# A perceiver layer on one core: split tail products, single-step layer norms, another setup, and a last group in two token halves

## The reference, cut to what matters

```python
x = x + xattn(_layernorm(x), ctx_768, ...)   # 16 heads of 64: q from x, k and v from the context
x = x + attn(_layernorm(x), ...)             # 16 heads of 16 inside a batch
x = x + ffn(_layernorm(x), ...)              # r * (relu(xk @ Wk.T)**2 @ Wv.T), r = sigmoid(xr @ Wr.T)
```

## Time and profile before

| what | value |
| --- | --- |
| median of three runs | 902.88 us |
| the profiled execution: own time, span in the trace | 905.87 us, 903.4 us |
| PE, weight loads | 822.6 us (91%), 641.3 us (71%) |
| DVE, ACT, POOL | 579.5 us (64%), 549.5 us (61%), 430.7 us (48%) |
| mean granted TensorE clock | 0.972 |
| first score, first score of group 1's part of the list | 44.98 us, 123.71 us |
| end of the last AC job on TensorE, end | about 826 us, 903.4 us |

### The profile page before, as it was taken

The page is one execution under the profiler, slowest core; times in us unless marked ns, Lnnn a source line. Parts: engine busy times, 40 slices in busy tenths (PEclk is TensorE's granted clock), DMA queues, the critical chain, the costliest instruction groups (busy, mean ns, idle before and its releaser), DMA issues.

```text
span 903.4 us, 20097 instructions
## 1 busy us (share of the span) xinstructions
PE 822.6 (91%) x7414; PEld 641.3 (71%) x7414; DVE 579.5 (64%) x1674; ACT 549.5 (61%) x1338; POOL 430.7 (48%) x661
## 2 busy tenths in 40 slices
PE   5699989998999989998999989998999999897653
PEld 3487758785878758786878768785878768684532
DVE  2553475769576775778576775778576756682344
ACT  1566865688467865677467865677467864673111
POOL 1036733755256723755266724755266724764001
PEclk9889999999999999999999999999999999999767
DMA  7301110001000110102010110002000110000000
GB/s 208 123 12 48 25 48 13 25 25 50 22 25 25 28 56 12 26 24 64 9 25 25 36 48 13 25 24 71 1 25 25 37 36 13 25 12 24 1 1 12
DMA packets 49232, 30.49 MB, mean 34 GB/s; under 512 B 22896, under 2 KB 48304, under 8 KB 49136
## 3 DMA queue, kind: packets, MB, share of 16 engines
q1 hardware_dynamic: 49136, 29.22, 11.9%
HBM read 26.85 MB, written 2.10 MB: 32 GB/s over the span
## 4 chain that ended last, share of the span: by engine, by line
PE 67%; DVE 14%; issue 7%; POOL 6%; ACT 5%; SPq 1%; DMA 1%; POOLq 0%; DVEq 0%; ACTq 0%
PE score L661 15%; PE post L755 5%; PE pre L573 5%; DVE qk_t L1123 5%; PE probT L670 4%; PE ac_tail L685 4%; POOL prT_l L356 4%; PE post L764 3%; DVE qk_l L1118 3%; PE ac_main L691 3%; PE ac_main L695 3%; PE aux L624 2%; PE ac_main L692 2%; PE post L738 2%; PE post L744 2%
## 5 line engine op out<-in xcount | busy, mean ns | idle before, releaser
L491 POOL TENSOR_SCALAR pr<-pr,rsum,poison 128x257 f32<-128x257 f32 x256 | 166.6, 660 | 233.6 <-DVE rsum L1148 233.5
L356 POOL TENSOR_TENSOR prT_l<-prT,prT_h 128x512 fp32r<-128x512 f32 x128 | 169.1, 1324 | 126.6 <-ACT prT_h L945 126.6
L928 ACT ACTIVATE pr<-sm,nmx 128x257 f32<-128x257 f32 x256 | 129.8, 509 | 83.8 <-DVE nmx L1142 83.4
L1142 DVE CUSTOM_DVE_ANT_0 sm<-score,mbias 128x257 f32<-128x257 f32 x256 | 106.2, 422 | 85.4 <-PE score L661 68.5
L937 ACT ACTIVATE prT<-probT 128x512 f32<-128x512 f32 x128 | 75.6, 590 | 44.9 <-PE probT L670 44.5
L661 PE MATMUL score<-cT_h,qk_h 128*128 128x258 f32 x256 | 89.6, 350 | 13.2 <-DVE qk_t L1123 12.9
L945 ACT ACTIVATE prT_h<-prT 128x512 fp32r<-128x512 f32 x128 | 80.7, 630 | 1.1
L670 PE MATMUL probT<-ident,pr 128*128 128x128 f32 x512 | 77.7, 274 | 3.4 <-POOL pr L491 2.6
L661 PE MATMUL score<-cT_h,qk_t 128*128 128x258 f32 x256 | 73.5, 287 | 0.0
L661 PE MATMUL score<-cT_l,qk_h 128*128 128x258 f32 x256 | 73.1, 285 | 0.0
L661 PE MATMUL score<-cT_h,qk_l 128*128 128x258 f32 x256 | 73.1, 285 | 0.0
(11 more groups left out here) (260 smaller groups left out, 2024.5 us busy)
## 6 DMA issues: line engine op xcount, KB each, us to landing
cx_in<-in_ctx_dram SPq DMA_DIRECT2D x64, 192.0 KB, 2.4
cx_in<-in_ctx_dram SPq DMA_DIRECT2D x64, 64.0 KB, 2.3
xn<-in_x_dram SPq DMA_DIRECT2D x8, 256.0 KB, 3.4
xb<-in_x_dram SPq DMA_DIRECT2D x8, 256.0 KB, 3.5
out_dram<-yo SPq DMA_DIRECT2D x8, 256.0 KB, 2.7
wq<-in_L_xattn_Wq_dram SPq DMA_DIRECT2D x1, 1024.0 KB, 5.1
wo<-in_L_xattn_Wo_dram SPq DMA_DIRECT2D x1, 1024.0 KB, 7.6
wqkv<-in_L_attn_W_qkv_dram SPq DMA_DIRECT2D x1, 768.0 KB, 8.8
```

What stands on the lines that cost most here:

```text
L356: eng.tensor_tensor(prT_l[:, :, cut], prT[:, :, cut], prT_h[:, :, cut], ALU.subtract).then_inc(prob_lower, 1)
L491: last = pool.tensor_scalar(p, p, rsum[:, j % 2, t:t + 1], poison[:, 0:1], ALU.mult, ALU.mult)
L928: act.activation(pr[j % 2][:, t, :], sm[:, t % 2, :], ACT.Exp, bias=nmx[:, j % 2, t:t + 1], scale=-1.0, accum_out=ssum[:, j % 2, t:t + 1]) ...
L1142: dve.tensor_tensor_reduce(sm[:, t % 2, :], score[t % 2][:, 0:NK], mbias[:], DH ** -0.5, BIG, ALU.add, ALU.min, nmx[:, j % 2, t:t + 1]).th ...
```

## The change

**Tails.** The tail channels are split as the main ones are. `c_hl` holds for each row 128 main channels (upper), 64 tail channels (upper), 64 tail channels (lower), 128 main channels (lower); its columns 128 to 255 are one stationary tile, so that a 512-column product gives the tail's upper part in the lower and its lower part in the upper 64 rows of ac_tail. ACT copies the rows 64 to 127 to `act_low`, and DVE adds the two in two pieces.

**Layer norm.** Twelve stages of one wait each, with a place in the list for each; the Newton step uses a scaled copy of the variance and takes one column at a time.

**Setup.** The transfers come in another order, small and large loads apart, the query weights in two halves. Products of the setup use further banks; the feed-forward weights are transposed in group 0 (`F0` to `F2`); K0 to K11 (there named `H`) stand in group 0's list among the first scores.

**Lists.** There are three of each: first group, middle groups, last group. In the last one the remainder of group 7 is cut in two token halves, `.0` (batches 0 to 3) and `.1`, with banks of their own. A product into a post bank waits for the last user of that bank.

```diff
+PE_LAST = (
...
+    "S2:7 S3:7 P1:6 AC:5 FR FK P0:7 AC:6 FV OT0.0 P1:7 OT1.0 WO.0 LT.1 AC:7 OT0.1 T2.0 OT1.1 QT.0 KT.0 WO.1 SC.0 VR.0 "
+    "T2.1 QT.1 KT.1 SC.1 VR.1 PT.0 PV.0 T4.0 PJ.0 PT.1 PV.1 T4.1 PJ.1 T3.0 T3.1 FR.0 FK.0 FR.1 FV.0 FK.1 FV.1").split()
...
-SETUP = "WK0 Q0 WK1 F0 Q1 WK2 F1 Q2 WK3 F2 Q3".split()
...
+SETUP = "WK0 WK1 XT WK2 WK3 Q0 LEFT Q1 CT0".split()
...
-LN_LINKS = 5 + 3 * NEWTON
+LN_LINKS = 5 + 2 * NEWTON
+LN_STAGES = LN_LINKS + 1
...
+        c_hl = [sb(f"c_hl{r}", [P, 2, 2 * DC], F32R) for r in range(2)]
+        UPPER, TAILS, LOWER = slice(0, P), slice(P, 2 * DC - P), slice(2 * DC - P, 2 * DC)
+        act_low = sb("act_low", [64, NH * NQ])
...
+        QK_SETUP_BANKS = [(score[0], score[1]), (post, probT), (ac_main, ac_tail), (post, probT), (ac_main, ac_tail), (post, pre)]
...
+        CLOSING_OT_BANKS = {"OT0.0": (post, pre), "OT1.0": (post, pre), "OT0.1": (score[0], score[1]), "OT1.1": (probT, ac_tail)}
+        CLOSING_BANKS = [(pre, post), (ac_main, aux, score[0], score[1], probT, ac_tail)]
...
+        SETUP_PRE_BANKS = {"XT": pre, "Q0": probT, "Q1": ac_main, "Q2": ac_tail, "Q3": pre}
...
             sp.dma_start(xn[:], token_rows(x_rows, 0)).then_inc(x_in, 16)
-            sp.dma_start(wq[:], Wq.rearrange("(k p) n -> p k n", p=P)).then_inc(wq_in, 16)
+            for n, v in ((G1, g1), (B1, be1)):
+                sp.dma_start(cols[:, n, :], column(v)).then_inc(ln1_in, 16)
...
-            for n, v in ((G1, g1), (B1, be1), (G2, g2), (B2, be2), (MUR, mur), (MUK, muk)):
+            wq_columns = Wq.rearrange("(k p) n -> p k n", p=P)
+            sp.dma_start(wq[:, :, 0:512], wq_columns[:, :, 0:512]).then_inc(wq_in, 16)
+            sp.dma_start(left_in[:, 0:DC], ctx_in[:, NKF, :]).then_inc(left_staged, 16)
+            sp.dma_start(left_in[:, DC:256], ctx_in[:, NKF, P:DC]).then_inc(left_staged, 16)
+            load_ctx(0, 0)
...
+            sp.dma_start(wq[:, :, 512:1024], wq_columns[:, :, 512:1024]).then_inc(wq_rest_in, 16)
...
             eng.wait_ge(c_upper, g * GB + j + 1)
-            eng.tensor_tensor(c_l[j % 2][:], cx_in[j % NCTX][:, :, 0:P], c_h[j % 2][:], ALU.subtract).then_inc(c_lower, 1)
+            c, src = c_hl[j % 2], cx_in[j % NCTX]
+            eng.tensor_tensor(c[:, :, DC:2 * P], src[:, :, P:DC], c[:, :, P:DC], ALU.subtract)
+            eng.tensor_tensor(c[:, :, LOWER], src[:, :, 0:P], c[:, :, UPPER], ALU.subtract).then_inc(c_lower, 1)
...
                 after(pe, acm_copied, g * GB + j)
                 after(pe, act_copied, g * GB + j)
 
-                pe.wait_ge(probT_copied, n)
-                for m in range(2):
-                    by_pair = prT[:, m, :].rearrange("p (n r x) -> p n r x", r=2, x=2 * NQ)
-                    for r in range(2):
-                        pe.matmul(ac_tail[r * 64:r * 64 + 64, 0:TOK], cx_in[j % NCTX][:, m, P:DC], by_pair[:, :, r, :],
-                                  start=(m == 0), stop=(m == 1))
                 pe.wait_ge(c_lower, g * GB + j + 1)
                 pe.wait_ge(prob_upper, n)
+                c = c_hl[j % 2]
                 for m in range(2):
-                    pe.matmul(ac_main[:], c_h[j % 2][:, m, :], prT_h[:, m, :], start=(m == 0), stop=False)
-                    pe.matmul(ac_main[:], c_l[j % 2][:, m, :], prT_h[:, m, :], start=False, stop=False)
+                    pe.matmul(ac_main[:], c[:, m, UPPER], prT_h[:, m, :], start=(m == 0), stop=False)
+                    pe.matmul(ac_main[:], c[:, m, LOWER], prT_h[:, m, :], start=False, stop=False)
+                    pe.matmul(ac_tail[:], c[:, m, TAILS], prT_h[:, m, :], start=(m == 0), stop=False)
                 pe.wait_ge(prob_lower, n)
                 for m in range(2):
-                    last = pe.matmul(ac_main[:], c_h[j % 2][:, m, :], prT_l[:, m, :], start=False, stop=(m == 1))
+                    pe.matmul(ac_main[:], c[:, m, UPPER], prT_l[:, m, :], start=False, stop=(m == 1))
+                    last = pe.matmul(ac_tail[:], c[:, m, TAILS], prT_l[:, m, :], start=False, stop=(m == 1))
                 last.then_inc(ac_done, 1)
...
                 act.wait_ge(probT_full, 2 * (g * GB + j) + half + 1)
...
-                    after(act, ac_done, g * GB + j)
+                after(act, prob_lower, 2 * (g * GB + j - 1) + half + 1)
                 act.activation(prT[:, :, half * 256:(half + 1) * 256], probT[:].rearrange("p (m c) -> p m c", m=2),
...
+                if half == 0:
+                    after(act, ac_done, g * GB + j)
                 cut = slice(half * 256, (half + 1) * 256)
                 act.activation(prT_h[:, :, cut], prT[:, :, cut], ACT.Copy).then_inc(prob_upper, 1)
...
-                act.activation(c_h[j % 2][:], cx_in[j % NCTX][:, :, 0:P], ACT.Copy).then_inc(c_upper, 1)
+                act.activation(c_hl[j % 2][:, :, 0:DC], cx_in[j % NCTX][:, :, 0:DC], ACT.Copy).then_inc(c_upper, 1)
 
             def weighed(g, j):
                 act.wait_ge(ac_done, g * GB + j + 1)
+                after(act, act_copied, g * GB + j)
+                act.activation(act_low[:], ac_tail[64:128], ACT.Copy).then_inc(tail_lower, 1)
                 act.activation(acm[:, :, j * NQ:(j + 1) * NQ], ac_main[:].rearrange("p (h q) -> p h q", q=NQ),
                                ACT.Copy).then_inc(acm_copied, 1)
...
+                w, y, q = lw[:, n, 0], lw[:, n, 1], lw[:, n, 2]
+                if stage > 0:
...
                 if stage == 0:
...
+                    for a in part:
+                        last = dve.bn_stats(st[:, n, a, :], src[:, a, :])
+                elif stage == 1:
...
-                    dve.bn_aggr(mv[:, n, 0, :], st[:, n, 0, :])
-                    dve.bn_aggr(mv[:, n, 1, :], st[:, n, 1, :]).then_inc(ln_link[n], 1)
-                elif stage < 4:
-                    if stage == 1:
-                        linked(2)
-                        dve.tensor_scalar(w, mv[:, n, :, 1], scale, shift, ALU.mult, ALU.add).then_inc(ln_link[n], 1)
-                        linked(3)
-                        dve.tensor_scalar(li[:, n, :], w.bitcast(I32), 1, None, ALU.logical_shift_right).then_inc(ln_link[n], 1)
-                        linked(4)
-                        dve.tensor_scalar(y.bitcast(I32), li[:, n, :], -1.0, RSQRT_SEED, ALU.mult, ALU.add).then_inc(ln_link[n], 1)
...
-                    dve.tensor_tensor(q, y, y, ALU.mult).then_inc(ln_link[n], 1)
-                    linked(i + 1)
-                    dve.scalar_tensor_tensor(out=q, in0=q, scalar=-0.5, in1=w, op0=ALU.mult, op1=ALU.mult).then_inc(ln_link[n], 1)
-                    linked(i + 2)
-                    dve.scalar_tensor_tensor(out=y, in0=q, scalar=1.5, in1=y, op0=ALU.add, op1=ALU.mult).then_inc(ln_link[n], 1)
...
+                elif stage == 2:
+                    dve.tensor_scalar(w[:, own], mv[:, n, own, 1], -0.5 * scale, -0.5 * shift, ALU.mult, ALU.add)
+                    last = dve.tensor_scalar(lw[:, n, 3, own], mv[:, n, own, 1], scale, shift, ALU.mult, ALU.add)
+                elif stage == 3:
+                    last = dve.tensor_scalar(li[:, n, own], lw[:, n, 3, own].bitcast(I32), 1, None, ALU.logical_shift_right)
+                elif stage == 4:
+                    last = dve.tensor_scalar(y[:, own].bitcast(I32), li[:, n, own], -1.0, RSQRT_SEED, ALU.mult, ALU.add)
...
+                elif stage % 2:
+                    for a in part:
+                        one = slice(a, a + 1)
+                        last = dve.scalar_tensor_tensor(out=q[:, one], in0=y[:, one], scalar=w[:, one], in1=y[:, one],
+                                                        op0=ALU.mult, op1=ALU.mult)
...
+                    last = dve.scalar_tensor_tensor(out=y[:, own], in0=q[:, own], scalar=1.5, in1=y[:, own], op0=ALU.add, op1=ALU.mult)
+                last.then_inc(link, 1)
...
-                dve.wait_ge(ac_done, g * GB + j + 1)
-                dve.tensor_copy(act_[:, :, j * NQ:(j + 1) * NQ],
-                                ac_tail[:, 0:TOK].rearrange("p (n q) -> p n q", q=NQ)).then_inc(act_copied, 1)
+                dve.wait_ge(tail_lower, g * GB + j + 1)
+                upper, lower = (t.rearrange("p (n r e q) -> p n r e q", r=2, e=2, q=NQ) for t in (ac_tail[0:64], act_low[:]))
+                for r in range(2):
+                    own = act_[r * 64:r * 64 + 64, :, j * NQ:(j + 1) * NQ].rearrange("p (n e) q -> p n e q", e=2)
+                    last = dve.tensor_tensor(own, upper[:, :, r], lower[:, :, r], ALU.add)
+                last.then_inc(act_copied, 1)
...
-                if j == 0 and t in FIRST_USE:
-                    pe.wait_ge(qk_split, g * N_QK + FIRST_USE[t])
+                first_use = FIRST_USE_0 if g == 0 else FIRST_USE
+                if j == 0 and t in first_use:
```

829 lines of the change are left out of this document (464 added, 365 removed), and 48 rows, old and new, of tables (ACT_FIRST, ACT_LAST, ACT_ORDER, DVE_FIRST).

## The result

The changed kernel takes 888.64 us (median of 4 runs, 886.88 to 890.68) against 902.69 (4 runs, 899.77 to 904.21): ratio 0.9854 [0.9833, 0.9874]. It is 1.5% faster, 14 us where 40 were forecast, and 863 lies 26 us too low. The profiled execution was the slowest of the four, 890.68 with a span of 888.6 (before: 905.87 and 903.4).

What follows compares the result with a forecast made beforehand. TensorE was taken to bound the middle, chains the start and end. From 905.87, -11.4 (tails), -7 (setup) and -23 (end) gave 864.5; median 861.5, plus 1.5 for waits: 863. Forecast 852 to 870 (chance 0.55), range with rivals 845 to 884.

Steps and rivals of the forecast that it cites:

- The tails: Weighing job (AC) after each score: ten 512-column products instead of mixed ones, 0.27 us less a batch, 1.6 a middle group.
- the lists and the layer norm: Middle groups: layer norm costed at 0; waits brought by other lists cost 0.2 us a group, 1.5 in seven groups.
- The lists also fill the waits: Rival: K products' 2.4 us of waits a group and the last group's 7.7 vanish; 845 us, chance 0.13.
- Slower: the longer copies hold TensorE: Rival: each AC job waits for longer copies, up to 1.6 us; 908 us at its middle, chance 0.06.
- H0 8.7 us sooner brings S3 8 us sooner: Setup: first key product at 21.5 instead of 30.2, batch 0's fourth score near 44; stage 8 us shorter, net -7.
- the waiting of that stage takes up about 3 of the 7.3: Last group: first half's OT and WO steps, 7.3 us, moved ahead of the last AC job; existing waits absorb about 3.
- the clock of the chain: Closing behind the last AC job: step-by-step chain of the second half, 52 us to the end, bounds 45 to 65.
- I leave them slow: Closing: products behind PT assumed to stay at the low clock; an estimated 4 us more gain at 2.4 GHz not counted.
- the shorter gaps of the halves might keep the clock: Closing: by the clock-gate rule, products behind PT could stay at 2.4 GHz, an estimated 4 us more gain, not counted.
- the ends bring half: Rival: setup gains 3 us and end 12, as halves meet on VectorE; 878 us, chance 0.24 shared with tails gaining nothing.

Runs made afterwards that it cites:

- the throw-away products: Changed kernel plus unread TensorE products: 13 in the setup, 886.5 us; 47 in the closing instead, 884.1 us.
- the one run that mended it: Kernel with last group in middle order and closing throw-away products (872.8 us), its closing lists reordered so one half's steps no longer follow the other's late ones: 874.6 us.

## Why the prediction was wrong

**The middle: the right way, and 3.3 us too little.** A group fell to 99.0 (99.5 forecast), AC to 2.28 (2.3), and the copies on ScalarE and VectorE were hidden. But the parts were not as told, so that the sum came near is in part luck. The tails give 1.1 a group, not 1.6; as much comes with the lists and the layer norm, which I had priced at a loss of 0.2. "The lists also fill the waits" was partly right: the K waits fell from 14.6 to 8.4. "Slower: the longer copies hold TensorE" was refuted for this change, yet the split in the old lists costs 18 us a group. That danger was real.

**The setup: the step that failed is that H0 8.7 us sooner brings S3 8 us sooner, and the end of the stage with it.** H0 came 8.4 us sooner, S3 0.1, the stage not at all. Up to 61 us, where the first AC job stands in both kernels (61.78 before, 60.80 after), TensorE is busy for the same time, before and after:

```profile
0.00:61.00 61.00, 42.62 (x255) 31.21 (x255) 28.02 (x94) 26.18 (x57) 7.25 (x25) 0.92 0.43 124
```

```profile
0.00:61.00 61.00, 42.56 (x259) 29.54 (x260) 28.39 (x97) 26.27 (x62) 10.39 (x32) 0.92 0.45 125
```

It is idle for 18.4 us in either: the idle time moved, and none of it went. The stage missed by 9.9 us, in three parts. One part is a misreading: the 52.27 that I took for S3 is S0 of batch 1, which with S3 at 44 would have stood at 45.2, 7 us sooner and not 8. The second is that S3 came at 49.07 instead of 44. Of these 5.1 us 3.9 are the clock, 0.76 between 30 and 50 us, as the throw-away products show (45.18). The third, 3.5 us, lies behind S0 of batch 1. Group 0 takes 87.1 us from there instead of 83.9, and 83.6 were forecast (83.9, 1.3 more for the feed-forward transposes, 1.6 less for the tails). Before, then after:

```profile
52.27:136.19 83.92, 78.10 (x620) 59.66 (x620) 44.78 (x145) 60.18 (x150) 43.98 (x75) 1.00 0.14 36
```

```profile
50.40:137.54 87.14, 77.98 (x597) 62.78 (x596) 52.09 (x175) 67.47 (x161) 45.74 (x77) 1.00 0.13 34
```

TensorE is busy for the same 78 us and idle for 9.2 instead of 5.8. What the first group's list waits for stays open: the waits for context loads, the largest named ones, gave nothing when one of them was taken away.

**The last group: the step that failed is that the waiting of that stage takes up about 3 of the 7.3.** I took the waiting from the order before and assumed the new order had it to spare. In the middle order the steps cost 6.1 instead of 4.3. The larger error is one that I had put at nothing: the order chosen for this group is itself 8.9 us longer than the middle order with the same steps, and that is most of the 12.3 missed. The rest, some 1.7, is the tails' 2.2, of which about 0.5 came. That an order for one group could be worse than the one beside it I had not made a rival.

**Behind the last AC job: the step that failed is the clock of the chain.** 52 was worked out step by step. I wrote "I leave them slow" of the products behind PT but added up steps at the fast rate for QT.1, KT.1 and SC.1 (3.76 us for QT.1 and KT.1 together, where T2.1, both and two copies were to take 3.5), though the slow level stands in the earlier trace rows. The chain then took 54.8 to 59.7 with the clock left free. At the full clock it takes 50.7; that this is near 52 is in part luck, since the 52 had slow products in it. The Trainium skill, page "TensorE: Matmul & The Clock Gate", section "The HAM clock gate", says that the array's default is throttled and that activity releases it. I had weighed that by this rule the shorter gaps of the halves might keep the clock: they did not, the granted clock was 0.50 from 850 to 870 us. With the throw-away products it was 1.00 over the whole closing, as the rule has it.

**The sum.** Misses of +9.9, -3.3, +12.3 and +7.7 make the 26.6 between 862 and 888.6 in the profile. The rival "the ends bring half" (878) had the right sign and named the halves' meeting on VectorE. That meeting is in the profile (C6.0 waited 5 us for PJ.1), but the one run that mended it gained nothing, so what it costs is not shown. What is shown is the order of the last group (8.1 us in the medians) and the clock of the closing (4.5 to 7.7) and of the setup (2.1 to 2.7). With these three edits the kernel takes 18.5 us less. The throw-away products are no part of the change, and they help the kernel before as well (6.6 us in its closing).

## What to carry to other kernels

An earlier milestone is no gain: compare the bounding engine's idle time up to a point at which both kernels have done the same work, name that point by its job and not by its place in the timeline, and price a stage by that. Work put "into waits" is free only if the order that it joins has those waits, so run the old order with the new steps in it before a new one. Where a chain of waits between engines sets the time of a closing, read the granted clock first, work out the chain at both levels, and try throw-away products in its gaps. Compare such closings by several executions, since their clock differs from one to the next.

## What the runs showed of the hardware

- Products whose results nobody reads, in the gaps of the closing, kept its granted clock at 0.97 to 1.00, where it was 0.69 to 0.83 without. They shortened two closings by 8.3 and 10.5 us and the one of the halves by 4 to 9, as its clock without them happened to be: 59.7 us at 0.69, 57.6 at 0.75, 54.8 to 55.6 at 0.83, 50.7 at 1.00.
- A VectorE operation of 128x1024 with two inputs from SBUF took 2.10 and, the next, 1.76 instead of 1.22 us beside GpSimd operations, of which the second, an addition, took 1.73 instead of 0.73. The Trainium skill, page "SBUF — State Buffer", section "SBUF: two separate sides", says that VectorE and GpSimd share one pair of ports, and that of a VectorE operation with two inputs from SBUF and a GpSimd operation that reads SBUF the one that starts first holds it for its whole instruction. The trace agrees: the multiplication on GpSimd started at 839.88, 0.02 us ahead of VectorE's, and was not slowed (1.05); VectorE's first ended at 842.00, 1.1 us behind the end of that multiplication, GpSimd's addition 0.6 us later, and VectorE's second another 1.1 us later.
